# Attention and the last stage in one block: the first pair of row tiles is mixed inside the last attention units

## The reference

```python
def xattn(x, cond):                      # x: 2048 rows of 512, cond: 4096 rows of 512
    q = fq(heads(x @ Wq + bq) / sqrt(32));  k = fq(heads(cond @ Wk + bk));  v = fq_columns(heads(cond @ Wv + bv))
    a = fq_unsigned(softmax(q @ k.T))    # 16 heads, every row against all 4096 keys
    return merge(a @ v) @ Wp + bp

def ffn(x):                              # bitlinear: rows to 8 bits, weights to -1, 0, 1
    h = gelu(silu(bitlinear(x, w1, b1))) # 512 -> 2048
    return bitlinear(layer_norm(h, ln_g, ln_b), w2, b2)

x = x + tanh(g_xattn) * xattn(layernorm(x), ctx)
return x + tanh(g_ffn) * ffn(layernorm(x))
```

## Time and profile before

| | |
|---|---|
| time before, median of 3 runs | 1856.4 us (1856.22 to 1860.22) |
| the profiled execution: its own time, its span | 1849.33 us, 1847.3 us |
| busy share of the span: PE, DVE, ACT, POOL | 85%, 90%, 77%, 71% |
| attention, first score matmul to the barrier | 294.85 to 1544.98 us |
| last stage | 1544.98 to 1847.3 us |
| mean granted TensorE clock | 0.961 |

### The profile page before, as it was taken

The page is one execution under the profiler, slowest core; times in us unless marked ns, Lnnn a source line. Parts: engine busy times, 40 slices in busy tenths (PEclk is TensorE's granted clock), DMA queues, the critical chain, the costliest instruction groups (busy, mean ns, idle before and its releaser), DMA issues. The chain is left out here.

```text
span 1847.3 us, 35476 instructions
## 1 busy us (share of the span) xinstructions
PE 1577.1 (85%) x13635; PEld 777.1 (42%) x13651; DVE 1666.4 (90%) x2239; ACT 1416.7 (77%) x1379; POOL 1310.9 (71%) x1293
## 2 busy tenths in 40 slices
PE   8799996888888988888888888888888886779984
PEld 4344441444444444444444444444444443323331
DVE  7788886998999999999999999999999993479894
ACT  5467777787889888889888887988888782677772
POOL 0144443898979989888988898898989896345530
PEclk9899996999999999999999999999999997889997
DMA  6746664989867899885798986678787874022313
GB/s 222 237 153 224 226 206 132 179 164 173 157 116 140 149 184 175 170 157 105 151 170 172 185 164 130 122 140 154 138 156 138 169 129 121 14 62 63 75 40 79
DMA packets 683721, 269.80 MB, mean 146 GB/s; under 512 B 610521, under 2 KB 641305, under 8 KB 682274
## 3 DMA queue, kind: packets, MB, share of 16 engines
q1 hardware_dynamic: 682178, 264.62, 67.2%
q0 software_dynamic: 704, 1.62, 0.2%
q10 hardware_dynamic: 672, 1.31, 0.2%
HBM read 84.20 MB, written 31.49 MB: 63 GB/s over the span
## 5 line engine op out<-in xcount | busy, mean ns | idle before, releaser
L911 DVE TENSOR_SCALAR_CACHE_REDUCE att_scaled<-att_scores,layer_nsq 128x1536 f32<-128x1536 f32 (+1 forms) x768 | 1200.3, 1636 | 16.8 <-PE att_scores L868 16.2
L931 POOL CAST att_probsT<-att_pairsT 128x2048 bf16<-128x2048 uint8 x512 | 954.8, 1894 | 96.5 <-DMA att_pairsT<-att_pairs 86.4
L982 ACT ACTIVATE att_pairs<-att_scaled,att_bias_row 128x4096 uint8<-128x4096 f32 x256 | 950.5, 3713 | 76.8 <-DMA att_pairsT<-att_pairs 47.6
L868 PE MATMUL att_scores<-first_k_head,first_q_head 96*128 96x512 bf16 x1024 | 297.1, 394 | 95.1 <-DVE att_scaled L911 75.8
L868 PE MATMUL att_scores<-att_k_head,att_q_head 96*128 96x512 bf16 x1024 | 285.8, 381 | 64.9 <-DVE att_scaled L911 59.1
L882 PEld LDWEIGHTS att_ps_o<-att_v_head,att_probsT 128*128 128x128 bf16 x8192 | 242.4, 96 | 69.1 <-POOL att_probsT L931 9.0
L882 PE MATMUL att_ps_o<-att_v_head,att_probsT 128*128 128x32 bf16 x8192 | 244.9, 176 | 6.3 <-ACT layer_o_sum L974 3.9
L868 PEld LDWEIGHTS att_scores<-first_k_head,first_q_head 96*128 96x128 bf16 x1024 | 81.3, 99 | 256.1 <-DVE att_scaled L911 172.8
L846 PE MATMUL att_scores<-att_k_head,att_q_head 96*128 96x512 bf16 x651 | 175.8, 379 | 0.0
L868 PEld LDWEIGHTS att_scores<-att_k_head,att_q_head 96*128 96x128 bf16 x1024 | 79.1, 97 | 210.3 <-DVE att_scaled L911 149.2
L846 PE MATMUL att_scores<-first_k_head,first_q_head 96*128 96x512 bf16 x600 | 167.1, 390 | 0.0
(11 more groups left out here) (163 smaller groups left out, 1727.2 us busy)
## 6 DMA issues: line engine op xcount, KB each, us to landing
layer_w2T<-ctx_T SPq DMA_DIRECT2D x96, 256.0 KB, 3.9
k_parts<-kv_k_stage SPq DMA_DIRECT2D x16, 768.0 KB, 5.1
q_w_in<-in_L_ffn_w_dram SPq DMA_DIRECT2D x32, 256.0 KB, 2.8
kv_weights_ctx_in<-in_ctx_dram SPq DMA_DIRECT2D x32, 256.0 KB, 5.1
kv_weights_w_in<-in_L_ffn_w_dram SPq DMA_DIRECT2D x32, 256.0 KB, 4.9
ctx_T<-kv_inT SPq DMA_DIRECT2D x8, 1024.0 KB, 6.0
att_k_head<-k_parts SPq DMA_DIRECT2D x96, 64.0 KB, 2.6
first_k_head<-k_parts SPq DMA_DIRECT2D x84, 64.0 KB, 2.8
```

The lines of the kernel that those rows point to most:

```text
L868: last = pe.matmul(buffer[:, x:x + 512], q_head[slot][:, at:at + P], k_head[slot][:, STARTS[j] + x:STARTS[j] + x + 512], start=True, stop= ...
L911: dve.tensor_scalar(scaled[u][:, STARTS[j]:STARTS[j] + WIDTHS[j]], scores[(g * NCH + j) % 2][:, 0:WIDTHS[j]], kept["nsq"][:, g:g + 1], Non ...
L931: pool.tensor_copy(probsT[g % C_BUFS][:, parity * HALF:(parity + 1) * HALF, :].rearrange("p k q -> p (k q)"), turned.rearrange("p (n two) ...
L982: act.activation(pairs[g % R_BUFS][:, :].bitcast(U8).rearrange("p (c two) -> p two c", two=2), scaled[u][:, :].rearrange("p (two c) -> p t ...
```

## The change

`attend` and `finish` become one function, `attend_and_finish`, with one block, so that the barrier between them goes. Round 0 of the last stage goes with it. Its work on pair 0 is written into the units 244 to 255 of the attention loop, at unit numbers set by hand. The products with the values of the last four units (252 to 255), which stood in five more passes of the attention loop, are written into round 1 of the last stage.

- Step 1, `x + gated bias`: made in the stage of the keys and values for all 16 row tiles (one load of 256 KB, one POOL addition, one store of 256 KB each), kept in a DRAM tensor `xb`, and loaded from there by the last stage. The gates and `bp` are loaded at the end of the first stage, tanh moves to the second. `add_bias` goes.
- Step 2, `wp`: loaded at unit 196, and scaled on ACT after the units 206 to 212 in place of DVE in the last stage.
- Step 3, pair 0: `invert_steps` of four row tiles on DVE at unit 246, `scale_out` on POOL at 244 and 246, `turn_out` and `project` of tiles 0 and 1 in ten places on PE that held three spare matmuls each (`EARLY_PE`; a product over one of four parts of `wp` in each of eight), `keep_out` on ACT at 246 and 250, `add_mixed` on DVE at 250 and 254, `negate_mean` on POOL at 249 and 253, `centre` on ACT at 251 and 254, `largest(0)` on DVE at 253.
- Step 4, behind the last unit: DVE goes on with `largest(1)`, `step_first(0)` and `quantise_first`, POOL puts `split_inverse(0)` between the two halves of the cast of unit 253, PE turns the integers of pair 0 after the product of unit 251, and ACT keeps those of tile 0 before the exponentials of unit 255.
- Step 5: `sum_weights` and what follows from it on DVE move from rounds 0 and 1 to round 2, the second bias goes to round 2, and buffers of the last stage lie in those of attention that are free by then (`rows` in `scaled`, `turned` in `pairs` and `pairsT`, `ps_h` in `scores`, one `outT` in place of two).

```diff
@@ project_keys_values
+        XB_LOAD, XB_ADD, XB_STORE = 2, 4, 6
...
+                    i = row_tile(g, XB_LOAD)
+                    if i is not None:
+                        after(sp, xb_stored[i % XB_BUFS], 16 * (i // XB_BUFS))
+                        sp.dma_start(xb[i % XB_BUFS][:, :], x_tiles[:, i, :]).then_inc(xb_loaded[i % XB_BUFS], 16)
+                    i = row_tile(g, XB_STORE)
+                    if i is not None:
+                        sp.wait_ge(xb_ready, i + 1)
+                        sp.dma_start(xb_tiles[:, i, :], xb[i % XB_BUFS][:, :]).then_inc(xb_stored[i % XB_BUFS], 16)
...
+                    i = row_tile(g, XB_ADD)
+                    if i is not None:
+                        pool.wait_ge(gated_ready, 1)
+                        pool.wait_ge(xb_loaded[i % XB_BUFS], 16 * (i // XB_BUFS + 1))
+                        pool.tensor_tensor(xb[i % XB_BUFS][:, :], xb[i % XB_BUFS][:, :], bp[:, :], ALU.add).then_inc(xb_ready, 1)
@@ attend_and_finish
+        WP_AT, WP_SCALE = 196, (206, 208, 210, 212)
+        EARLY_LOADS, EARLY_TILES = (242, 243), 4
+        EARLY_PE = {(247, 0): (0, None), (248, 0): (0, 0), (248, 2): (0, 1), (249, 0): (0, 2), (249, 2): (0, 3),
+                    (250, 2): (1, None), (252, 0): (1, 0), (252, 2): (1, 1), (253, 0): (1, 2), (253, 2): (1, 3)}
...
+                    if g == UNITS - 3:
+                        sp.dma_start(b1_rows, t["b1_rows"]).then_inc(b1_loaded, 16)
+                        load_x(2)
+                        load_x(3)
+                        sp.dma_start(ln_b, t["L0_ffn_ln_b"].partition_broadcast(P)).then_inc(norm_loaded, 16)
...
+                pe.wait_ge(fin_const, 2)
+                weigh(UNITS - 5)
+                for i in pair_of(0):
+                    turn_ints(i)
...
+                        if r == 1:
+                            weigh(UNITS - 4 + 2 * i)
...
+                    if g == 246:
+                        keep_out(0)
+                    if g == 250:
+                        keep_out(1)
+                    if g == 251:
+                        centre(0)
+                    if g == 254:
+                        centre(1)
+                    if g == UNITS - 1:
+                        keep_ints(0)
+                    exponentials(g)
...
+                    if g == 244:
+                        scale_out(0)
+                    if g == 246:
+                        scale_out(1)
+                    if g == 249:
+                        negate_mean(0)
+                    if g == 253:
+                        negate_mean(1)
+                        invert_sd(0)
+                lowest(UNITS - 1)
+                unpack_half(UNITS - 3, 0)
+                split_inverse(0)
+                scale_out(2)
...
+                for g in range(UNITS):
+                    if g == 246:
+                        invert_steps(0, EARLY_TILES)
+                    if g == 250:
+                        add_mixed(0)
+                    if g == 253:
+                        largest(0)
+                    if g == 254:
+                        add_mixed(1)
```

More of the change, by code:

```diff
@@ L1150, in _, with keep_clock, value_chunk @@
             def _(pe):
-                pe.wait_ge(const, 2)
+                def keep_clock(unit, slot, at, times):
+                    spare = scores[unit % 2][:, WIDTHS[2]:WIDEST]
+                    for _ in range(times):
+                        pe.matmul(spare, q_head[slot][:, at:at + P], k_head[slot][:, 0:C], start=True, stop=True)
+                def value_chunk(group, j, k):
+                    n = chunk_index(group, j, k)
+                    pe.wait_ge(chunk_loaded[n % RING], 16 * (n // RING + 1))
+                    if k == 0:
+                        after(pe, block_kept, block_index(group, j))
+                    pe.matmul(ps_v[:, :], wp[:, k, group * P:(group + 1) * P], ctx_chunk[n % RING],
+                              start=(k == 0), stop=(k == CT - 1)).then_inc(chunk_done, 1)
@@ new lines, in weigh @@
+                def weigh(r):
+                    h = r // QT
+                    if r % QT == 0:
+                        pe.wait_ge(v_turned[h % 2], 16 * (h // 2 + 1))
+                    pe.wait_ge(probs_ready, r * PIECES + PIECES)
+                    after(pe, o_kept, r)
+                    for k in range(KT):
+                        last = pe.matmul(ps_o[:, 0:D], probsT[r % C_BUFS][:, k, :],
+                                         v_head[h % 2][:, k * D:(k + 1) * D], start=(k == 0), stop=(k == KT - 1))
+                    last.then_inc(pv_ready, 1)
@@ new lines, in early_work, with step @@
+                def early_work(i, k):
+                    if k is None:
+                        turn_out(i)
+                    else:
+                        project(i, k, k + 1)
+                def step(g, s):
+                    slot, at = s // QT, (s % QT) * P
+                    if live(g, UNITS) and s % QT == 0:
+                        after(pe, kq_loaded[slot], ((g >> 5) + slot) * KQ_LOADS)
+                    for j in range(NCH):
+                        if live(g, UNITS):
+                            buffer = scores[(s * NCH + j) % 2]
+                            after(pe, scaled_ready, g * NCH + (j - 1))
+                            for x in range(0, WIDTHS[j], 512):
+                                last = pe.matmul(buffer[:, x:x + 512], q_head[slot][:, at:at + P],
+                                                 k_head[slot][:, STARTS[j] + x:STARTS[j] + x + 512], start=True, stop=True)
+                            last.then_inc(scores_ready, 1)
+                        if j == 0 and live(g, UNITS) and chunk_of(g):
+                            value_chunk(*chunk_of(g))
+                        elif j == 0 and live(g, UNITS):
+                            if (g, j) in EARLY_PE:
+                                early_work(*EARLY_PE[g, j])
+                            elif live(g - V_LAG, UNITS):
+                                keep_clock(g - 1, slot, at, 3)
+                        if j == 1 and live(g - V_LAG, UNITS):
+                            weigh(g - V_LAG)
+                        if j == 2 and live(g - V_LAG, UNITS):
+                            if (g, j) in EARLY_PE:
+                                early_work(*EARLY_PE[g, j])
+                            else:
+                                keep_clock(g, slot, at, 3)
@@ L1169, in turn_ints @@
+                for g in range(UNITS):
+                    step(g, g % UNROLL)
                 def turn_ints(i):
@@ new lines, in invert_steps @@
+                def invert_steps(first, stop):
+                    steps = den[:, :].rearrange("p (h i) -> p h i", i=QT)[:, :, first:stop]
+                    done = 0 if first == 0 else 2
+                    dve.wait_ge(pairs_ready, UNITS - QT + stop)
+                    dve.reciprocal(steps, steps).then_inc(p_step_ready, 1)
+                    dve.wait_ge(p_step_ready, done + 1)
+                    dve.tensor_scalar(steps, steps, 1e-8, None, ALU.max).then_inc(p_step_ready, 1)
+                for g in range(UNITS):
+                    if g == 246:
[6 more added lines that the diff above has]
+                        add_mixed(1)
+                    if g % GROUP_UNITS == SCALE_AT and g // GROUP_UNITS + 1 < GROUPS:
+                        scale_group(g // GROUP_UNITS + 1)
+                    u = g % S_BUFS
+                    after(dve, pairs_ready, g - S_BUFS + 1)
+                    for j in range(NCH):
+                        dve.wait_ge(scores_ready, g * NCH + (j + 1))
+                        dve.tensor_scalar(scaled[u][:, STARTS[j]:STARTS[j] + WIDTHS[j]], scores[(g * NCH + j) % 2][:, 0:WIDTHS[j]],
+                                          kept["nsq"][:, g:g + 1], None, ALU.mult, ALU.min,
+                                          accum_out=low[u][:, j:j + 1]).then_inc(scaled_ready, 1)
@@ L1483, in _ @@
+                largest(1)
+                step_first(0)
+                for i in pair_of(0):
+                    quantise_first(i)
+                invert_steps(EARLY_TILES, QT)
+                for r in range(1, PAIRS + 3):
                     mixed, normed, done = pair_of(r), pair_of(r - 2), pair_of(r - 3)
```

667 lines of the change are left out of this document (323 added, 344 removed).

## The result

The changed kernel takes 1846.8 us (median of 6 runs, 1840.8 to 1849.5) where the kernel before takes 1858.8 beside it: a ratio of 0.9916, interval 0.9891 to 0.9942. Measured once more it was 1843.8 against 1859.9, ratio 0.9908 (0.9888 to 0.9927). The gain is 12 to 16 us; 25.5 were forecast.

What follows compares the result with a forecast made beforehand. Attention was taken as paced by VectorE (busy 1200.3 us, waiting 16.8), with no engine full at the join. 29.7 - 4.5 + 2.0 - 1.7 = 25.5 us less, so 1856.4 - 25.5 = 1831; range 1821 to 1842.

Steps and rivals of the forecast that it cites:

- The join: From VectorE's last scaling to the feed-forward part's first product: 11.5 us against 46.2; 8.3 or 15.5 in other cases.
- The long step that I had named: After attention, `step_first`, on two numbers in SBUF, may be held off until POOL's half cast ends, then takes 1.1 us.
- Rounds 1 and 2: Last stage: round 1, 31.7 us before, gets 4.5 us longer; round 2 gets 2.0 us shorter.
- the collision: POOL's small step held by VectorE's L1446 moves from round 2 to round 1: 2.0 us paid there, 2.0 back.
- The second stage: Keys and values: 16 POOL additions fit a 2.56 us gap, costing 0.5; stage and its two edges 1.7 us.
- That rival (0.13): POOL's additions collide with VectorE in the keys and values stage: 14.7 us instead of 0.5, 1845; half, 1838; chance 0.13.
- this edge: Ahead of the keys and values stage, `bp` and the gates load before `wv`: 256 KB, 0.7 us.
- VectorE inside attention ... Sum 4.6 us: Attention loop: two `add_mixed` at 1.69 us each, `largest` 0.65, `invert_steps` 0.6; all 4.6 us on the path.
- VectorE's last scaling therefore ends at 1526.24 + 4.6 + 0.4 = 1531.2: End of attention: the old end plus 4.6 us on VectorE and 0.4 on TensorE, with no stall from POOL or ScalarE.
- The term of 0.4 us for TensorE inside attention: Ten places in attention: quarter products replace spare matmuls, 0.28 us more under 0.49 of slack; 0 to 3 us, 0.4 taken.
- The rival "doesn't fit": Early work in attention makes TensorE late and VectorE stands: 1 us a place gives gain 16, 1840; 1.5 gives 1845; chance 0.10.
- the first of the signs that the prediction gave for being wrong: Attention: VectorE waits for scores in the last ten units.

Runs made afterwards that it cites:

- second profile: The changed kernel profiled a second time, no edit: VectorE waits 37.3 us and attention takes 1256.5 us.
- early loads: Each head's key and query loads start four units earlier: kernel before 1843.8 us (0.9915), changed kernel 1823.5 us (0.9801).
- packed: Changed kernel with its three new small tiles in unused ends of sv, v_inv and bv, later SBUF tiles at old addresses: 1840.2 us, ratio 0.989.

## Why the prediction was wrong

**The join was right, and a little better.** 9.2 us against 11.5 counted, inside the bounds of 8.3 to 15.5. The long step that I had named is there: L1526, on 128x2 numbers, takes 1.82 us and ends at 1556.87, POOL's cast beside it at 1556.85. What was too dear is the way to it: I had POOL at the last `lowest` 2 us after VectorE's end, and it was there at once, so the half cast ended 2.7 us after VectorE and not 4.6. The steps behind it took 6.5 us against 6.9.

**Rounds 1 and 2 were right.** Round 1 is 34.9 us (31.7 + 4.5 = 36.2 forecast), round 2, from its first product at 1598.20 to that of round 3 at 1629.07, is 30.9 where it was 33.2 (2.0 less were forecast), and the collision moved as said: in round 1 of the changed kernel POOL's L1417, on two numbers, is held by VectorE's product of 2048. In round 2, and in all later ones, no member of `split_inverse` takes over 0.34 us, as against the earlier trace rows.

```profile
1592.34 2.34 DVE L1543 SCALAR_TENSOR_TENSOR att_scaled<-att_scaled,att_mean_neg,att_head_area 128x2048 f32<-128x2048 f32 x1
1592.55 2.18 POOL L1417 TENSOR_TENSOR att_inv_rest<-att_inv_rest,att_inv_parts 128x2 f32<-128x2 f32 x1
```

**The second stage: right on the additions, low on the edges.** They fit the gap; taking them out gave about 1 us. That rival (0.13) is excluded. But attention starts 0.7 to 3.7 us later in the pairs of profiles, against 1.7, and the first matmul of the stage starts 1.5 to 1.9 us later (89.85 against 88.32 in the first pair). For this edge the sum had 0.7 us, "256 KB at that rate"; at the rate of the earlier trace rows, 1024 KB in 12.1 us, 256 KB would be 3.0, so the term didn't follow from its row.

**"VectorE inside attention ... Sum 4.6 us" was low by about 1, and by chance.** The new work of the early tiles is 5.7 us in the first profile; `invert_steps` is the part that was off, 1.76 where I took 0.6 (2.0 was the upper bound):

```profile
1499.76 3.73 POOL L1375 CAST att_probsT<-att_pairsT 128x2048 bf16<-128x2048 uint8 x2
...
1501.73 0.55 DVE L1592 RECIPROCAL layer_den<-layer_den 128x64 f32<-128x64 f32 x1
1502.32 1.21 DVE L1594 TENSOR_SCALAR layer_den<-layer_den 128x64 f32<-128x64 f32 x1
```

In the second profile POOL's cast has just ended when the same step starts, and it takes 0.20 us:

```profile
1502.27 0.20 DVE L1594 TENSOR_SCALAR layer_den<-layer_den 128x64 f32<-128x64 f32 x1
```

In the first profile the reciprocal runs beside the cast in 0.55 us. The step behind it, from the same tile, ends at 1503.53, as the cast does (1503.49). With early loads it is 1.57 us beside a cast. It is the same holding off that I had priced for `step_first`, and had not looked for here. The Trainium skill, page "SBUF — State Buffer", section "Who interferes with whom", names `tensor_scalar` among the operations of VectorE that can enter a 2-port mode, in which they and GpSimd's exclude each other, and doesn't name the reciprocal. The traces agree for the one (1.21 and 1.57 us beside a cast, 0.20 without), and show the other not held (0.55).

**The step that failed is "VectorE's last scaling therefore ends at 1526.24 + 4.6 + 0.4 = 1531.2".** It ended at 1554.15. The sentence takes for granted that the 16.8 us of waits in attention stay 16.8; they were 34.5. They are not a constant. For the most part they are late key loads: with the loads four units earlier they fall to 10.1 us in the kernel before and to 13.3 in the changed one. The earlier trace rows only shows them as a sum, and I did not look where they stand. What raised them is shown in part. The execution had few of them by chance: 27.8 us in the next one of the same kernel. The tiles moved by 96 bytes, which the diff shows as three harmless lines: in the kernel before shifts of 32 and 64 bytes there cost about 9 us, in the changed kernel packing gave about 4 back, by intervals that overlap. And the load of Wp at unit 196 isn't in the sum at all, although it is a moved transfer of 1 MB; packed, the wait at head 13 goes from 4.1 to 0.4 us without it, and the time doesn't change. How much each has of the 17.7 us stays open. With the key loads given room the gain is 20 to 24 us of the 25.5.

**The term of 0.4 us for TensorE inside attention** also failed, in most executions. Its working, 0.28 us more under a slack of 0.49, came true in the first profile, where the clock stayed at 1.00. In the early-load profile units 244 to 255 take 9.1 us more than before, of which 6.0 are VectorE's new work; some 3 us are left for this term, the upper bound given for it.

**The rival "doesn't fit"** named the right symptom, VectorE waiting for scores. In the first profile of the changed kernel it does not happen where the early work is; in the second and with early loads it does, 1.7 and 2.5 us, which is the first of the signs that the prediction gave for being wrong. That the measured gain of 12 to 16 us comes near its price of 16 is luck: most of the miss lies at the changes of head.

## What to carry to other kernels

A wait that is small in the profile and repeats at regular places is a race that the slow side only just wins: read where it stands and which load is late, and give that load its earliest start before anything is laid on top. Profile the kernel before twice before a sum is made on one execution. Where new work replaces matmuls that only keep TensorE busy, look at the granted clock of that stretch in more than one profile of the changed kernel. When new tiles are added, put them behind the others or into unused ends, and time a version with nothing but the tile added.

## What was not expected of the hardware

An unused tile of 32 or 64 bytes ahead of w1T and w2T costs 0.5% of the time (1.0054 and 1.0047); 64 bytes behind them cost nothing (0.9995 to 0.9997). What about the address does it stays open: multiples of 64 are not it, and which of the tiles it is was not separated.

A step of VectorE on two numbers (L1526) takes 1.82 us beside a cast of POOL, and one on 64 numbers (L1594) 1.21 to 1.57 us beside a cast and 0.20 without.
